# Routed expert tiles of a transformer block: the eight row transposes interleaved with the tail rows' down matmuls

## What is computed

```python
h = rmsnorm(x, rms_weight)
topv, topi = top_k(softmax(h @ router_w), 2)        # 8 experts, 2 per token
g = einsum('td,edf->tef', h, w_gate)                # F = 512
u = einsum('td,edf->tef', h, w_up)
eo = einsum('tef,efd->ted', silu(g) * u, w_down)
out = x + einsum('te,ted->td', w_dense, eo) + shared_expert(h)
```

## Time and profile before

| | |
|---|---|
| median of 3 runs (lowest, highest) | 635.94 us (635.56, 636.33) |
| span of the profiled execution, first to last instruction | 633.0 us |
| own time of the profiled execution | not given; the median lies 2.9 us above its span |
| TensorE matmul busy | 611.9 us, 97% |
| VectorE, ScalarE, GpSimd busy | 83%, 67%, 23% |
| eight routed passes | from 383.4 to 597.9 us of the span, about 26.8 us each |

### The profile page before, as it was taken

How to read it: one execution, slowest core, us unless ns; L and a number is a source line. 1 busy time by engine, 2 the same in 40 slices (tenths; PEclk the granted TensorE clock), 3 DMA queues, 4 the chain that set the end, 5 groups by cost and what they waited for, 6 DMA issues and landing times.

```text
span 633.0 us, 10577 instructions
## 1 busy us (share of the span) xinstructions
PE 611.9 (97%) x3624; PEld 475.4 (75%) x3625; DVE 524.0 (83%) x886; ACT 421.6 (67%) x558; POOL 148.1 (23%) x167
## 2 busy tenths in 40 slices
PE   8899999998999999999989999999999999999996
PEld 6678888887886444444557888898988989889775
DVE  5888888878787777889999479789797988979686
ACT  4998888889755989784574366639376483855630
POOL 2354446416000333527920310000000000000051
PEclk9999999999999999999999999999999999999999
DMA  8977776765246997936999558796775968759257
GB/s 337 420 291 298 301 303 238 310 267 191 100 174 260 403 362 286 400 134 241 402 364 416 216 204 325 262 370 224 299 315 200 390 210 319 273 219 393 86 176 264
DMA packets 31070, 177.91 MB, mean 281 GB/s; under 512 B 4064, under 2 KB 4064, under 8 KB 14784
## 3 DMA queue, kind: packets, MB, share of 16 engines
q1 hardware_dynamic: 25536, 158.64, 65.3%
q0 software_dynamic: 5504, 18.88, 8.2%
HBM read 154.30 MB, written 23.20 MB: 280 GB/s over the span
## 4 chain that ended last, share of the span: by engine, by line
PE 50%; DVE 19%; ACT 14%; issue 8%; DMA 5%; POOL 2%; DVEq 1%; POOLq 0%; ACTq 0%; SPq 0%
PE BK L2132 10%; PE BK L306 9%; DVE WL L1029 4%; ACT RA L1383 4%; ACT PR L1410 4%; PE BK L2135 3%; PE BK L1882 3%; PE BK L312 3%; PE BK L318 3%; PE BK L313 3%; DMA RA<-wbit 2%; PE BK L2102 2%; PE BK L1827 2%; DMA RX<-wbit 1%; PE BK L2155 1%
## 5 line engine op out<-in xcount | busy, mean ns | idle before, releaser
L2132 PE MATMUL BK<-EX,WH 128*128 128x320 f32 x384 | 101.3, 344 | 0.3
L1029 DVE TENSOR_TENSOR WL<-RA,WH 128x2048 fp32r<-128x2048 f32 x40 | 89.4, 2287 | 7.6 <-ACT WH L1586 7.4
L2135 PE MATMUL BK<-EX,WL 128*128 128x160 f32 x336 | 79.3, 236 | 0.0
L1586 ACT ACTIVATE WH<-RA 128x2048 fp32r<-128x2048 f32 x40 | 73.6, 1910 | 0.2 <-PE BK L1925 0.2
L2132 PEld LDWEIGHTS BK<-EX,WH 128*128 128x128 f32 x384 | 69.7, 188 | 1.9 <-DVE SR L1069 1.9
L2135 PEld LDWEIGHTS BK<-EX,WL 128*128 128x128 f32 x336 | 64.1, 191 | 0.0
L705 POOL DMA_INDIRECT GA<-rows,SLOT x4 | 4.9, 1229 | 240.4 <-DVE WL L1029 239.5
L652 POOL TENSOR_TENSOR HB<-HB,ND (+2 forms) x26 | 28.6, 1121 | 100.5 <-DVE BH L915 99.9
L1482 ACT ACTIVATE RA<-RA,RT 128x2048 int16<-128x2048 f32 x22 | 43.7, 1998 | 3.8 <-DMA RA<-wbit 1.9
L1029 DVE TENSOR_TENSOR WL<-RC,WH 128x2048 fp32r<-128x2048 f32 x20 | 45.0, 2285 | 0.7 <-ACT WH L1586 0.7
L1882 PE MATMUL BK<-TG,XQ 128*128 128x512 bf16 x192 | 42.4, 379 | 0.1
(11 more groups left out here) (328 smaller groups left out, 1644.1 us busy)
## 6 DMA issues: line engine op xcount, KB each, us to landing
RA<-wbit SPq DMA_DIRECT2D x54, 1024.0 KB, 6.7
RA<-wmoe SPq DMA_DIRECT2D x40, 1024.0 KB, 6.5
RC<-wmoe SPq DMA_DIRECT2D x20, 1024.0 KB, 8.0
rows<-ZERO POOLq DMA_DIRECT2D x40, 256.0 KB, 8.2
XG<-rows SPq DMA_DIRECT2D x10, 512.0 KB, 3.7
rows<-YS SPq DMA_DIRECT2D x9, 512.0 KB, 6.0
RA<-wqk SPq DMA_DIRECT2D x7, 640.0 KB, 7.8
RA<-wo SPq DMA_DIRECT2D x4, 1024.0 KB, 7.5
```

Source lines behind the costliest of these rows:

```text
L1029: e.tensor_tensor(WL[m][:, q * RAW:q * RAW + RAW], RC[j][:, :], WH[m][:, q * RAW:q * RAW + RAW].bitcast(f32), ALU.subtract)\
L1586: e.activation(WH[m][:, q * RAW:q * RAW + RAW], RC[2 * m + q][:, :], ACT.Copy)\
L2132: mm = e.matmul(bank[GBK[f]][:, 0:2 * R], WH[m][:, at], EX[:, k, :, :].rearrange("p a b -> p (a b)"), start=k == 0, stop=k == KD - 1)
L2135: e.matmul(bank[GBK[f]][:, 0:R], WL[m][:, at], EX[:, k, 0, :], start=False, stop=False)
```

## The change

Each pass of `routed_tile` issues the same matmuls and transposes in another order. The first half of the tail rows' down matmuls (inner blocks k = 0 and 1, both output halves q, eight matmuls) moves ahead of the full rows' down products, directly behind the last up block. The eight transposes of the next tile's rows no longer stand in a row there: one goes behind each of these eight matmuls. `et_pe` is still signalled with the fourth and the eighth transpose. The second half of the tail matmuls (k = 2 and 3) stays at the end. All waits that stood around the transposes and ahead of the first down products come together ahead of the first tail matmul, except `ht_hi` of the second half and `free_c[5]`; added is a wait for the first `ht_lo`, because tail rows k = 0, 1 now need their low part there. VectorE computes that low part earlier: `routed_hidden_lo` is called once for each half q, q = 0 between the products f = 2 and f = 3, q = 1 where the whole stood, and the tail subtraction of 128x128 becomes two of 128x64. ScalarE, SyncE and GpSimd are unchanged.

```diff
@@ VectorE, routed_product and routed_hidden_lo
                     if n != 1:
                         ins.then_inc(s("eh"), 1)
+                    else:
+                        routed_hidden_lo(t, 0)
-            def routed_hidden_lo(t):
-                for q in range(2):
-                    ks = slice(2 * q, 2 * q + 2)
-                    e.wait_ge(s("ht_hi"), t * 2 + q + 1)
-                    ins = e.tensor_tensor(HX[:, ks, R + TAIL_R:2 * R], SR[:, ks, 0:P], HX[:, ks, 0:P].bitcast(f32),
-                                          ALU.subtract)
-                    if q == 0:
-                        ins.then_inc(s("ht_lo"), 1)
-                e.tensor_tensor(HX[:, :, R:R + TAIL_R], SR[:, :, P:R], HX[:, :, P:R].bitcast(f32), ALU.subtract)\
+            def routed_hidden_lo(t, q):
+                ks = slice(2 * q, 2 * q + 2)
+                e.wait_ge(s("ht_hi"), t * 2 + q + 1)
+                e.tensor_tensor(HX[:, ks, R:R + TAIL_R], SR[:, ks, P:R], HX[:, ks, P:R].bitcast(f32), ALU.subtract)
+                e.tensor_tensor(HX[:, ks, R + TAIL_R:2 * R], SR[:, ks, 0:P], HX[:, ks, 0:P].bitcast(f32), ALU.subtract)\
                     .then_inc(s("ht_lo"), 1)
@@ VectorE, tile
-                routed_hidden_lo(t)
+                routed_hidden_lo(t, 1)
@@ TensorE
+            def tails(h, rows=None):
+
+                def row_block(n):
+                    if rows is not None:
+                        m = e.transpose(bank[TB[n // 4]][:, n % 4 * P:n % 4 * P + P], rows[:, n * P:n * P + P], IDF[:, :])
+                        if n % 4 == 3:
+                            m.then_inc(s("et_pe"), 1)
+                for q in range(2):
+                    for k in (2 * h, 2 * h + 1):
+                        n = 4 * q + 2 * (k % 2)
+                        if k:
+                            e.matmul(bank[6 + q][XTAIL, :], HX[:, k, P:R], WL[2][:, down_at(k, q)], start=False, stop=False)
+                            row_block(n)
+                        mm = e.matmul(bank[6 + q][0:2 * TAIL_R, :], HX[:, k, P:R + TAIL_R], WH[2][:, down_at(k, q)],
+                                      start=k == 0, stop=k == KE - 1)
+                        row_block(n if k == 0 else n + 1)
+                        if k == 0:
+                            e.matmul(bank[6 + q][XTAIL, :], HX[:, k, P:R], WL[2][:, down_at(k, q)], start=False, stop=False)
+                            row_block(n + 1)
+                return mm
@@ TensorE, routed_tile
-                waits(e, ("hsum", t * 5 + 3))
-                routed_rows(t + 1)
-                waits(e, ("ys_a", t + 1), ("ys_d", t + 1), (free_c[4], gi + 1), (free_c[5], gi + 1))
-                for h in range(2):
-                    waits(e, ("ht_hi", t * 2 + h + 1))
-                    for q in range(2):
-                        highs(... k in (2 * h, 2 * h + 1) ..., h == 0)
+                waits(e, ("hsum", t * 5 + 3), ("ht_lo", t * 2 + 1), ("ys_a", t + 1), ("ys_d", t + 1), (free_c[4], gi + 1),
+                      ("e_in", t * 32 + 64))
+                tails(0, XG)
+                for q in range(2):
+                    highs(... k in (0, 1) ...)
+                waits(e, ("ht_hi", t * 2 + 2), (free_c[5], gi + 1))
+                for q in range(2):
+                    highs(... k in (2, 3) ..., False)
                 e.wait_ge(s("ht_lo"), t * 2 + 2)
                 for q in range(2):
                     lows(...)
-                for q in range(2):
-                    for k in range(KE):
-                        ... (the 16 tail matmuls)
+                mm = tails(1)
                 mm.then_inc(s("y2_pe"), 1)
```

More of the change, by code:

```diff
@@ L2139, in routed_tile @@
                             mm.then_inc(s("gate_pe"), 1)
-                waits(e, ("hsum", t * 5 + 3))
-                routed_rows(t + 1)
-                waits(e, ("ys_a", t + 1), ("ys_d", t + 1), (free_c[4], gi + 1), (free_c[5], gi + 1))
-                for h in range(2):
-                    waits(e, ("ht_hi", t * 2 + h + 1))
-                    for q in range(2):
-                        highs(e, bank[AB[q]], [(HX[:, k, 0:P], WH[2][:, down_at(k, q)], WL[2][:, down_at(k, q)])
-                                               for k in (2 * h, 2 * h + 1)], h == 0)
+                waits(e, ("hsum", t * 5 + 3), ("ht_lo", t * 2 + 1), ("ys_a", t + 1), ("ys_d", t + 1), (free_c[4], gi + 1),
+                      ("e_in", t * 32 + 64))
+                tails(0, XG)
+                for q in range(2):
+                    highs(e, bank[AB[q]], [(HX[:, k, 0:P], WH[2][:, down_at(k, q)], WL[2][:, down_at(k, q)]) for k in (0, 1)])
+                waits(e, ("ht_hi", t * 2 + 2), (free_c[5], gi + 1))
+                for q in range(2):
+                    highs(e, bank[AB[q]], [(HX[:, k, 0:P], WH[2][:, down_at(k, q)], WL[2][:, down_at(k, q)]) for k in (2, 3)],
+                          False)
                 e.wait_ge(s("ht_lo"), t * 2 + 2)
```

## The result

The changed kernel takes 641.58 us (median of 4 runs, 640.67 to 642.68) against 635.8 us for the kernel before (median of 4): a ratio of 1.0089, 95% interval 1.0073 to 1.0105, that is 4.6 to 6.7 us slower. Forecast were 642.2 us and +6.3. The span of its profiled execution is 640.2 us, where 639.3 was forecast. In the changed kernel the lines of this stage are: transposes 2100, tail matmuls 2107, 2109, 2113, up and gate products 2151 (before 2132), ScalarE's evacuations 1638 and 1640 (1640, 1642) and weight roundings 1584 (1586).

The account below looks back on a forecast made before the run. It took the kernel to be bound by a ring through TensorE, ScalarE and VectorE, closed by the gate_sum wait. Seven shifts of 0.90 us gave +6.3, all else 0: 642.2 us (+1.0%), range 638.7 to 645.2.

Parts of the forecast that it names:

- the ring: Routed passes: TensorE's transposes, ScalarE's roundings, VectorE's subtractions and gate_sum, then TensorE's next up products; claimed to set the 26.8 us period.
- the seven short waits: Up block f = 0, every pass but the first: TensorE's weight load waits for VectorE's gate_sum, about 0.3 us.
- (a): Transposes one by one between tail matmuls: claimed 0.11 us each, as in a row, so TensorE saves nothing.
- (b): Tail matmuls among the transposes: ScalarE's second evacuation and all behind it, then VectorE, claimed 0.90 us later per pass.
- t0: End of TensorE's up products in a pass, where its next instruction starts; the forecast counts times from it.
- The cover of 0.95 us: Before the change: time from the second transpose signal, t0 + 1.06, to ScalarE's start on that bank, t0 + 2.01.
- (c): VectorE's early half of the low part, between products f = 2 and f = 3: claimed to fit its idle 1.13 us.
- (d): Waits gathered ahead of the first tail matmul: costed at 0, up to 0.2 us, plus weight loads showing 0.2.
- (e): SyncE's row loads, waiting for the second et_pe, go from 428.0 to about 429.8: claimed cost 0.
- Seven crossings: Between each pass and the next: the 0.90 us shift enters the ring once, seven times, 6.3 us in all.
- a covered end: Behind the eighth pass: VectorE waits for the tail matmuls from 597.1 to 598.19, so 0.90 us was claimed covered.
- The sum: Whole kernel: 6.3 us more, span 633.0 to 639.3; with the median 2.9 above the span, 642.2 us.

Follow-up runs that it names:

- e5: Kernel before, with ScalarE's first weight rounding of the next expert moved into its idle stretch between the hidden product's halves: 634.58 us, ratio 0.9975.
- e7: Kernel before, with VectorE's gate_sum of the next pass moved ahead of the last of six subtractions: 633.87 us, ratio 0.9966.
- e4: Changed kernel, with ScalarE's first weight rounding of the next expert moved into its idle stretch between the hidden product's halves: 634.78 us, ratio 0.9981.
- e6: Changed kernel, with VectorE's gate_sum of the next pass moved ahead of the last of six subtractions: 634.35 us, ratio 0.9974.
- e8: Changed kernel, with two transposes behind each of the first four tail matmuls and ScalarE's first weight rounding moved early: 634.23 us, ratio 0.9965.
- e3: Changed kernel, with two transposes behind each of the first four tail matmuls instead of one behind each of eight: 636.16 us, ratio 1.0005.
- e9: Changed kernel, with the eight transposes in a row behind six of the first eight tail matmuls: 638.57 us, ratio 1.0046.
- e2: Changed kernel, with the eight transposes in a row behind the first eight tail matmuls: 641.78 us, ratio 1.0099.
- e1: Changed kernel, with the eight transposes back in a row ahead of the first eight tail matmuls: 636.11 us, ratio 1.0001.

## Why the prediction was right

- **What bounds the kernel.** Right, and shown from both sides: breaking the ring at ScalarE's end or at VectorE's makes the kernel before faster (e5, e7) and takes the change's whole loss away (e4, e6), with TensorE's order untouched. The Trainium skill ("Perfetto Trace Analysis", Identifying the Most-Contended Engine) has the engine with the highest occupancy optimised first, but says that matmul busy time measures TensorE badly and names its FLOP utilisation and the busy share of its weight loads instead. This case agrees: the weight loads' share is 75% where VectorE has 83%, and 89% beside 87% in a routed pass, so TensorE stands out only by its 97% of matmul time. The edit on TensorE lost, and two edits on engines at 83% and 67% gained; the seven short waits were the better guide.
- **(a) A transpose costs 0.11 us in either place.** Right to 0.01. The 8-column matmuls were the right neighbours: what limits an fp32 transpose here is not its weight load; whether it is the streaming of its columns, as the prediction said, no run separates. The Trainium skill's figures ("TensorE: Matmul & The Clock Gate", Back-to-back issue gap), by which 56 ns would have been left, do not hold for these fp32 columns: starts 0.34 us apart with 0.23 for the matmul leave 0.11. (The same section has 81 ns for 128 columns in a stream of loads and matmuls; the 108 ns of the transposes in a row do not agree with that either.) "Saves nothing" holds to 0.03 us a pass: the block is 0.02 to 0.03 longer one by one (e4) than in pairs (e8), in one trace each.
- **(b) The shift.** 0.90 was forecast. The second evacuation was expected at t0 + 2.91 and came at t0 + 2.94, the first rounding at + 3.7 and came at + 3.74; the shift is 0.94. The cover of 0.95 us is confirmed by e3 (all of it used, nothing lost) and e9 (half as much beyond it, half the loss). The step that was left out shows only there and in e2: a late first signal delays the second evacuation too.
- **(c), (d), (e): costed at nothing.** Right together: e1 keeps (c) and (d) and is equal to before within 0.15%; e4 keeps (e), with the row loads at t0 + 3.08 as in the changed kernel, and loses nothing. VectorE's early half took 0.55 us of 1.13, TensorE passed the gathered waits without a gap (first tail matmul 0.18 us behind the last up matmul, as the transposes before). But "costs nothing" had less room than the 0.4 us it was given: `ht_lo` came 0.48 us ahead of t0, and in e6, with 0.33, the load behind the gathered waits was already late.
- **Seven crossings and a covered end.** Right: seven waits. Behind the eighth pass VectorE's copy of the result starts with no idle time before it where it had 1.11. That cover is used up to the last tenth: VectorE's timeline there in the changed kernel is

```profile
600.36 4.49 DVE L1029 TENSOR_TENSOR WL<-RA,WH 128x2048 fp32r<-128x2048 f32 x2 [1.21 <-ACT WH L1584]
604.91 0.69 DVE L1125 COPY YS<-BK 128x512 f32<-128x512 f32 x1
```

- **The sum.** 7 x 0.94 = 6.6 in the trace, 5.8 between the medians, 6.3 forecast; the interval of the ratio, 4.6 to 6.7 us, holds the forecast and the trace's 6.6. The weakest number in it was TensorE's own need, taken as 26.5 from a stall of 0.3; it is 26.53 with the transposes in a row or in pairs; one by one it is about 26.56, an estimate from e4's 26.59 less the 0.03 it still waits. It did not enter the sum, because the ring was longer in both kernels. The level has a little luck in it. The 2.9 us between median and span was kept from before, but every run whose own time is known, of either kernel, takes only 1.7 to 1.9 us more than its span, so the profiled execution before was, by estimate, about 1.1 us faster than the median. So the span was forecast 0.9 too low and the median 0.6 too high; the difference of 6.3 does not depend on it.

## What to carry to other kernels

When one engine is busy 97% and still waits a few tenths of a microsecond at the same place in every pass, follow that wait back around: it may close a ring through other engines that sets the period, and then only the ring's links count. Before spreading out a block of instructions whose last one signals, measure the cover, the time between that signal and its taker's start: inside it spreading is free, beyond it every tenth is paid once per pass. The cheap repair was not on the busiest engine: one rounding moved into ScalarE's idle stretch, or one sum moved ahead of a subtraction, gave 0.25 to 0.35%. And when two bounds lie as close as ring and TensorE here, a variant that removes one wait can leave a trace of it or uncover another (e4, e6), so a difference of hundredths between such variants is not yet a price.

## What was not expected of the hardware

An fp32 transpose of 128 columns takes 0.11 us of TensorE in a row, in pairs and alone between 512-column matmuls, so hiding its weight load gains nothing; a bf16 transpose takes half of that the earlier trace rows. Strict alternation costs 0.02 to 0.03 us in eight transposes against pairs (e4 and e8), too little for the measured times to show.
